# A graph layer on one core: results 13 steps behind their group instead of 17, dense stores issued by ScalarE, and 4/9 of a step in each lookup turn

## The chip, the cores and the metric

The kernel runs on one core of a Trainium2 chip. The time is the device time of one execution in microseconds (us); of several runs the median is given. A profile of one execution shows what each engine did: TensorE (PE, its weight loads PEld), VectorE (DVE), ScalarE (ACT), GpSimd (POOL) and SyncE (SP), whose queue (SPq) only issues transfers here. All transfers share the core's DMA engines.

## The reference

One graph layer on 100,000 nodes of 128 numbers with 25,000 edges, followed by a layer norm over all nodes. Only nodes that own an edge get anything beside `x + x`.

```python
# src, dst: 25000 node numbers each; the layer's own dst is src, its src is dst
edge_feat = concatenate([h[dst], h[src], rel_pos, distance], axis=-1)
x = silu(edge_feat @ W1 + b1)
x = silu(x @ W2 + b2)
scores = (x @ W3 + b3)[:, 0]
mx = segment_max(scores, dst); exp_scores = exp(scores - mx[dst])
den = segment_sum(exp_scores, dst)
alpha = exp_scores / (den[dst] + EPS)
msg = h[src] @ Wv * (alpha * node_weight[src])[:, None]
out = segment_sum(msg, dst)
return layernorm(x + (h + out))
```

## The kernel before

The work has a dense and a sparse side.

**Dense.** All 100,000 rows are normalised as if no node had an edge. They come in 98 blocks of 1024 rows (`xin`, a ring of 8 blocks of 512 KB), two in each turn: SP loads a block (`load_block`, L323, which waits until the block that held the place has been stored), DVE takes its statistics (L969) at the end of a turn, a chain of 11 small DVE operations after every second turn (L930 to L951) makes scale and bias for four blocks, two turns later ACT (L510, 7 of a block's 8 rows per partition) and DVE (L990, the eighth) apply them, and SP stores the block (`store_block`, L332, after both).

**Sparse.** The edges are sorted by owner first (until about 105 us), then they are worked in 49 groups of 512. For 43 of them a lookup on PE finds sender and edge features of each sorted place (24 matmuls, L713, then 8 small ones, L700, between which DVE picks with L1018); the other 6 are fetched by GpSimd. GpSimd issues all indirect transfers in a fixed order, four for each piece: owner rows (`hk`), records of the 6 groups (`rt`), sender rows (`rec`, L443 for all), and last the scatters of the finished results (L447). The first scatter waits for all dense stores (`dense_written`, at turn 53), since a scatter overwrites dense rows; the scatter of a group waits for its result (`res_ready`, ACT L559). Sender rows pass through `rec` (a ring of `HS_RING` groups), are written out by SP (`write_rec`, L347) and come back by `load_rec` (L353) as `region`; the gather of group g waits until the group that held its place has been written out.

**Order.** Everything is written out by hand as turns, numbered from 0. Turns 0 to 42 hold one lookup each; turns 0 to 51 also hold dense work. A step s has three parts on each engine; it moves up to 18 groups one stage on: group s is transposed, s-1 meets `W1`, s-2 meets `W2`, s-3 is scored, and after the softmax of a batch of 4 groups its weights (`M_LAG`), sums (`Z_LAG`), rows (`Y_LAG`) and results follow. From turn `E_FROM` on each lookup turn takes one part of a step, later turns take a whole step. So step 11 begins in turn 43, and there are 99 turns for 67 steps. `bank[6]` of PSUM is shared: PE's small transpose (L665) waits for ACT's copy of the senders (L520). After the last turn edges that cross a tile are mended (`fix`), with two last scatters (L451).

Of the kernel before, what the change touches and what calls it, by code (L numbers as in the profile page):

```python
# [12 lines left out]
P = 128  # L13
# [14 lines left out]

HS_RING, R_RING, X_RING = 4, 12, 8
HK_SEMS, SC_SEMS, Y_SEMS, FAR_RING = 16, 8, 4, 4  # L30
KROW_RING = 2
ACT_ROWS = 7

BATCH = 4
BT = BATCH * TPG
NBATCH = -(-G // BATCH)
Y_LAG, Z_LAG, M_LAG, KROW_LAG = 12, 10, 9, 8
LAST_STEP = 67

# [5 lines left out]
REC_LAG = 7  # L45
E_FROM = 10
PARTS = 3
# [27 lines left out]
def turn_plan():  # L75

    plan, left, turn = [], [(s, p) for s in range(LAST_STEP) for p in range(PARTS)], 0
    while left:
        now = []
        if E_FROM <= turn < LOOKS:  # L80
            now.append(left.pop(0))
        elif turn >= LOOKS:
            now.append(left.pop(0))
            while left and left[0][0] == now[0][0]:
                now.append(left.pop(0))
        plan.append(now)
        turn += 1
    return plan
# [5 lines left out]
def looks(g):  # L94

    return sum(1 for v in LOOKED if v <= g)


# [15 lines left out]
def gnn_kernel(nc, x, xw, rec5, snd_tab, ef_tab, rcv_nat, id_nat, signs, iota, rowid, colid, word, w16d, w1, b1, w2, b2, w3, b3,  # L114
# [11 lines left out]
    with ExitStack() as ctx:  # L126
# [171 lines left out]
        def chain_turn(b):  # L298
            return batch_end(b) + Y_LAG + 1

        def res_turn(g):
            return max(chain_turn(batch_of(g)) + 1 + g % BATCH, g + Y_LAG + BATCH + 1)


        @block.sync
        def _(sp):
# [13 lines left out]
            def load_block(j):  # L320
                if 0 <= j < NB:
                    wait_ring(sp, stored, j - X_RING, 16)
                    sp.dma_start(xin[:, j % X_RING], x[rows_of(j), :].rearrange("(p r) h -> p r h", p=P)  # L323
                                 ).then_inc(x_in[j % X_RING], 16)

            def store_block(j):
                if 0 <= j < NB:
                    wait(sp, "norm_a", j + 1)
                    wait(sp, "norm_d", j + 1)
                    if j == NB - 1:  # L330
                        wait_ring(sp, stored, j - 1, 16)
                    sp.dma_start(out[rows_of(j), :].rearrange("(p r) h -> p r h", p=P), xin[:, j % X_RING]  # L332
                                 ).then_inc(stored[j % X_RING], 16)

# [51 lines left out]

            for i, now in enumerate(TURNS):
                store_block(2 * (i - 3) + 1)
                if i + 1 < LOOKS:
                    load_places(i + 1)  # L390
                for g in range(G):
                    if looks(g) - 1 + REC_LAG == i:
                        write_rec(g)
                if i == E_FROM - 1:
# [16 lines left out]
                if i >= 3:  # L411
                    load_block(2 * (i + 1))
                store_block(2 * (i - 2))
                if i >= 3:
# [88 lines left out]
        def _(act):  # L503
            def norm(i, half):
                j = 2 * (i - 2) + half
                if 0 <= j < NB:
                    wait(act, "chain_d", (j // 4 + 1) * STEPS)
                    for n in range(ACT_ROWS):
                        c = j % 4 * BR + n
                        ins = nc.scalar.activation(xin[:, j % X_RING, n, :], xin[:, j % X_RING, n, :], ACT.Identity,  # L510
                                                   bias=drs[:, j // 4 % 2, 1, c:c + 1], scale=drs[:, j // 4 % 2, 0, c:c + 1])
                    ins.then_inc(S["norm_a"], 1)
# [13 lines left out]
            def hidden(s):  # L526
# [7 lines left out]
                for b in range(NBATCH):  # L534
                    if batch_end(b) + 4 == s:
# [4 lines left out]
            def results(s):  # L540
                g = s - Z_LAG
# [4 lines left out]
                for b in range(NBATCH):  # L546
                    if batch_end(b) + 5 == s:
                        n = group_tiles(b)
                        wait(act, "alphaT_done", b + 1)
                        wait(act, "acol_ready", b - 1)  # L550
                        nc.scalar.activation(alT[:, b % 2, 0:n], bank[6][:, 0:n], ACT.Copy).then_inc(S["alT_ready"], 1)
                for g in range(G):
                    if res_turn(g) == s:
# [7 lines left out]
                        ins.then_inc(S["res_ready"], 1)  # L561

            for i, now in enumerate(TURNS):
                norm(i, 0)
                for s, part in now:
                    (turned, hidden, results)[part](s)
                norm(i, 1)

# [10 lines left out]
        def _(pe):  # L579
# [79 lines left out]
            def small_turns(s):  # L659
# [6 lines left out]
                for b in range(NBATCH):  # L666
                    if batch_end(b) + 5 == s:
# [23 lines left out]
            def turns(s):  # L691
                if s + 1 < G:
                    turn_rows(s + 1)
                    turn_senders(s + 1, sum(batch_end(b) + 5 <= s for b in range(NBATCH)))

# [45 lines left out]
        def _(dve):  # L741
# [220 lines left out]
            def dense_stats(i):  # L962
# [10 lines left out]
                if i % 2 == 1 or i == NPAIR - 1:  # L973
# [3 lines left out]
                    def gate():  # L977
                        wait(dve, "norm_a", 4 * (k - 1))
                        wait(dve, "norm_d", 4 * (k - 1))

# [3 lines left out]
            def dense_norm(i):  # L984
                for j in (2 * (i - 2), 2 * (i - 2) + 1):
                    if 0 <= j < NB:
                        wait(dve, "chain_d", (j // 4 + 1) * STEPS)
                        for n in range(ACT_ROWS, BR):
                            c = j % 4 * BR + n
# [102 lines left out]
            def part_two(s):  # L1092
                for b in range(NBATCH):
                    if chain_turn(b) == s:
                        def gate(b=b):
                            wait(dve, "res_ready", batch_end(b - 2) + 1 if b >= 2 else 0)

                        running.append(chain(("y_stats", batch_end(b) + 1), group_tiles(b), est[:, b % 2], ers[:, b % 2], cwe,
                                             "chain_e", b * STEPS, gate))
                    if batch_end(b) + 4 == s:  # L1100
                        softmax_first(b)
                    if batch_end(b) + 6 == s:
                        wait(dve, "alT_ready", b + 1)
# [4 lines left out]
                        dve.wait_ge(S["acol_ready"], b + 1)  # L1108

            def part_three(s):  # L1110
                if 0 <= s - M_LAG < G:
                    weights(s - M_LAG)
                more(3)
                for b in range(NBATCH):
                    if batch_end(b) + 4 == s:
                        softmax_second(b)
                more(99)
                if s == batch_end(NBATCH - 1) + 5:
                    dve.sem_inc(S["parts_ready"], 1)

            for i, now in enumerate(TURNS):
                if 0 <= i - 1 < LOOKS:
                    take_places(i - 1)
                one_hot(i, 0, EARLY)
                for b in range(NBATCH):
                    if (batch_end(b) + 4, 0) in now:
                        take_scores(b)
                if 0 <= i - 1 < LOOKS:
# [118 lines left out]
```

## Time and profile before

| | us |
|---|---|
| median of 3 runs (1011.95 to 1016.06) | 1012.76 |
| the profiled execution | 1010.98 |
| its span | 1009.2 |

The page of the profile gives the share of the span in which each engine was busy: PE 73%, DVE 65%, POOL 59%, ACT 52%, weight loads 49%. TensorE's clock was granted 0.892 of full on the mean. The profile moved 188.47 MB, mean 187 GB/s. The busy shares are means over very different stretches: sorting with DVE alone to about 105 us, lookups with dense work to about 562 us, steps with dense work to about 665 us, steps alone, and a tail of scatters. An engine's line says how long it was busy and who ended its idle time; for SP only its queue's waits are known. The program takes 1.78 us beyond its span.

### The profile page before, as it was taken

The numbers are of one execution on the slowest core, as the hardware profiler recorded it, in microseconds if no ns is written. First come the engines' busy times: TensorE is split into PE (matmuls) and PEld (weight loads), VectorE is DVE, ScalarE is ACT, GpSimd is POOL, SyncE is SP. The second block draws the span as 40 slices with busy tenths as digits, with TensorE's granted clock in tenths as the row PEclk, the third lists the DMA queues.
The fourth block names the chain that finished last, engine by engine and source line by source line (L and its number), as shares of the span: only waits on it lengthen the run. The fifth ranks groups of instructions, "written<-read, shape, count | busy, mean of one in ns | idle before, by whom it ended". The sixth has DMA issues, their size and how long they took to land.

```text
span 1009.2 us, 13449 instructions
## 1 busy us (share of the span) xinstructions
PE 735.5 (73%) x3718; PEld 493.6 (49%) x3718; DVE 655.5 (65%) x2314; ACT 527.1 (52%) x1230; POOL 596.9 (59%) x624
## 2 busy tenths in 40 slices
PE   0001688889878878797889786799999999996700
PEld 0000355555555545564556454566766666665600
DVE  8988789877766757676787666544355535547741
ACT  0000066566555645555556576876566666664630
POOL 3000777777777777777774337717644444446677
PEclk9999988989987878888898988899999999998755
DMA  6000369999889979979999869533322222222131
GB/s 215 0 0 5 78 186 315 336 344 344 288 269 320 327 217 331 329 223 291 356 321 321 247 208 304 168 117 101 92 80 83 80 83 85 83 65 66 65 80 45
DMA packets 120371, 188.47 MB, mean 187 GB/s; under 512 B 21147, under 2 KB 80182, under 8 KB 120296
## 3 DMA queue, kind: packets, MB, share of 16 engines
q1 hardware_dynamic: 100648, 148.85, 45.5%
q0 software_dynamic: 19648, 38.74, 13.8%
q8 instruction: 31, 0.51, 0.2%
q14 instruction: 44, 0.36, 0.1%
HBM read 109.89 MB, written 77.76 MB: 186 GB/s over the span
## 4 chain that ended last, share of the span: by engine, by line
PE 41%; DVE 19%; POOL 15%; issue 8%; DMA 8%; ACT 6%; SPq 2%; POOLq 0%; DVEq 0%; ACTq 0%
PE bank L713 9%; POOL rec L443 6%; POOL hk L443 6%; PE bank L680 4%; PE bank L687 4%; PE bank L643 4%; PE bank L655 4%; PE bank L634 3%; DMA xin<-in_x 3%; POOL out_rows L447 3%; PE bank L652 3%; PE bank L653 3%; ACT xin L510 3%; DVE region L776 3%; PE bank L700 2%
## 5 line engine op out<-in xcount | busy, mean ns | idle before, releaser
L510 ACT ACTIVATE xin<-xin,drs 128x128 f32<-128x128 f32 x686 | 269.4, 480 | 268.8 <-DVE drs L951 268.8
L447 POOL DMA_INDIRECT out_rows<-hk,sidx_t x196 | 192.4, 982 | 155.6 <-ACT hk L559 83.8
L713 PE MATMUL bank<-hk 128*125 128x512 bf16 x1032 | 267.5, 422 | 8.3 <-DVE snd_i L1026 5.4
L443 POOL DMA_INDIRECT hk<-in_x,kg_t x196 | 186.4, 951 | 143.5 <-DVE kg_t L860 84.0
L443 POOL DMA_INDIRECT rec<-in_xw,snd_i x196 | 185.5, 947 | 96.3 <-issue 56.7
L713 PEld LDWEIGHTS bank<-hk 128*125 128x125 bf16 x1032 | 156.7, 154 | 115.1 <-issue 40.6
L969 DVE BATCH_NORM_STATS2 dst<-xin 128x6 f32<-128x256 f32 x392 | 135.6, 413 | 32.8 <-DMA xin<-in_x 32.5
L1011 DVE TENSOR_SCALAR hk<-hk,rid 128x512 bf16<-128x512 f16 x344 | 110.0, 381 | 0.5 <-DMA hk<-vc_d 0.3
L1078 DVE TENSOR_TENSOR hk<-bank,hk 128x512 f32<-128x512 f32 x49 | 33.6, 687 | 102.1 <-PE bank L680 102.1
L700 PE MATMUL bank<-wsel,hk 125*128 125x5 f32 x344 | 52.4, 276 | 59.1 <-DVE hk L1018 59.1
L700 PEld LDWEIGHTS bank<-wsel,hk 125*128 125x128 f32 x344 | 48.6, 218 | 73.2 <-DVE hk L1018 71.7
L559 ACT ACTIVATE hk<-hk,ers 128x128 f32<-128x128 f32 x196 | 79.5, 482 | 0.4 <-DVE ers L951 0.4
L530 ACT ACTIVATE x<-bank,bcol 128x512 f32<-128x512 f32 x49 | 33.6, 686 | 66.5 <-PE bank L655 66.5
L586 PE MATMUL bank<-ident,region 128*128 128x128 f32 x8 | 2.7, 445 | 86.8 <-DVEq L792 86.8
L655 PEld LDWEIGHTS bank<-efT,w 16*128 16x128 f32 x392 | 47.2, 186 | 37.2 <-issue 37.2
L680 PE MATMUL bank<-wvh,zs 128*128 128x128 f32 x392 | 59.6, 300 | 6.8 <-ACT zs L545 3.4
L545 ACT ACTIVATE zs<-bank 128x512 f32<-128x512 f32 x49 | 29.0, 591 | 64.7 <-PE bank L687 64.7
L1069 DVE TENSOR_SCALAR m_q<-krow,kcol,acol 128x128 f32<-128x128 bf16 x196 | 57.1, 348 | 7.4 <-DMA krow<-seg_d 6.4
L1018 DVE SCALAR_TENSOR_TENSOR hk<-hk,cid,bank 125x512 f32<-125x512 f16 x43 | 31.9, 742 | 44.7 <-PE bank L713 44.7
L643 PE MATMUL bank<-x,w2s 128*128 128x512 f32 x98 | 60.9, 706 | 0.0
L687 PE MATMUL bank<-m_q,region 128*128 128x128 f32 x392 | 57.8, 296 | 0.0
L680 PEld LDWEIGHTS bank<-wvh,zs 128*128 128x128 f32 x392 | 52.6, 208 | 9.6 <-ACT zs L545 6.0
(203 smaller groups left out, 1020.7 us busy)
## 6 DMA issues: line engine op xcount, KB each, us to landing
xin<-in_x SPq DMA_DIRECT2D x98, 512.0 KB, 6.8
out_rows<-xin SPq DMA_DIRECT2D x98, 512.0 KB, 7.5
rec_d<-rec SPq DMA_DIRECT2D x49, 258.0 KB, 5.6
region<-rec_d SPq DMA_DIRECT2D x49, 258.0 KB, 3.4
hk<-vc_d SPq DMA_DIRECT2D x43, 256.0 KB
krow<-seg_d SPq DMA_DIRECT2D x49, 128.0 KB, 3.3
hk<-in_x,kg_t POOLq DMA_INDIRECT x196, 5.5
rec<-in_xw,snd_i POOLq DMA_INDIRECT x196, 6.0
```

The costliest lines, as they stand in the source:

```text
L443: pool.indirect_dma_start(out=to, out_offset=None, in_=frm, in_offset=bass.IndirectOffsetOnAxis(ap=index, axis=0)).then_inc(done, 16)
L447: pool.indirect_dma_start(out=out, out_offset=bass.IndirectOffsetOnAxis(ap=index, axis=0), in_=frm, in_offset=None).then_inc(done, 16)
L510: ins = nc.scalar.activation(xin[:, j % X_RING, n, :], xin[:, j % X_RING, n, :], ACT.Identity, bias=drs[:, j // 4 % 2, 1, c:c + 1], scale= ...
L559: ins = nc.scalar.activation(hk[:, g, q, :], hk[:, g, q, :], ACT.Identity, scale=ers[:, b % 2, 0, n:n + 1], bias=ers[:, b % 2, 1, n:n + 1])
L643: pe.matmul(bank[2][:], w2s[:], x1[:], start=True, stop=True).then_inc(S["mm2_done"], 1)
L655: ins = pe.matmul(bank[1][:, q * P:(q + 1) * P], w16[:, q, :], efT[:, g % 2, :], start=False, stop=(q == TPG - 1), skip_group_check=True)
L680: ins = pe.matmul(bank[4][:, q * P:(q + 1) * P], zs[:, q * P:(q + 1) * P], wvh[:], start=True, stop=True)
L687: ins = pe.matmul(bank[5][:, q * P:(q + 1) * P], rr[:, g % R_RING, q, 0:H], m_q[:, g % 2, q, :], start=True, stop=True)
L700: ins = pe.matmul(bank[7][:, q * WORDS:(q + 1) * WORDS], sel[0:SEL, q * P:(q + 1) * P], wsel[0:SEL, :], start=True, stop=True)
L713: ins = pe.matmul(bank[7][0:SEL, :], tab[:, k, n, 0:SEL], oh[:, k, :], start=(k == 0 and n == 0), stop=(k == CH - 1 and n == PIECES - 1))
L969: ins = vec.bn_stats(dst[:, c:c + 2, :].rearrange("p j w -> p (j w)"), xin[:, j % X_RING, n:n + 2, :].rearrange("p j h -> p h j"))
L1011: ins = vec.tensor_scalar(pair(oh[:, k, :]), vt[:, u % 2, :, 0, :], rid[:, k:k + 1], None, ALU.is_equal)
```

## The change

- `ACT_ROWS = 7` goes; `act_rows(j)` gives ACT all 8 rows of the blocks that are normalised in lookup turns (blocks 0 to 81) and 5 of the others (82 to 97); DVE does the rest, so none in lookup turns. The counts that wait for DVE's rows follow (`shared`).
- The dense stores move from SP to ACT's queue (`store`): the odd block's after ACT's first half of the next turn, the even block's after the turn's parts.
- SP writes the records out (`write_rec`) in turn g+7, behind the first of the turn's two block loads, no longer in turn looks(g)+6 at its beginning; `HS_RING` is 6, not 4.
- Steps begin in turn 9, and every third lookup turn takes two parts. 45 parts (15 steps) lie in lookup turns where 33 (11 steps) lay; step 15 begins in turn 43; 88 turns in all for 60 steps.
- All lags behind a group's scores are two steps shorter, softmax and what follows it one step earlier; the results come 13 steps behind their group, not 17, those of the last two batches at once.

```diff
-HS_RING, R_RING, X_RING = 4, 12, 8
+HS_RING, R_RING, X_RING = 6, 12, 8
-ACT_ROWS = 7
-Y_LAG, Z_LAG, M_LAG, KROW_LAG = 12, 10, 9, 8
-LAST_STEP = 67
+Y_LAG, Z_LAG, M_LAG, KROW_LAG = 10, 8, 7, 6
+LAST_STEP = 60
-E_FROM = 10
+E_FROM = 9
         if E_FROM <= turn < LOOKS:
             now.append(left.pop(0))
+            if (turn - E_FROM) % PARTS == PARTS - 1:
+                now.append(left.pop(0))
+def act_rows(j):
+    return BR if j // 2 + 2 < LOOKS else 5
+def shared(j):
+    return sum(1 for k in range(j + 1) if act_rows(k) < BR)
...
-            return batch_end(b) + Y_LAG + 1
+            return batch_end(b) + Y_LAG
...
-            return max(chain_turn(batch_of(g)) + 1 + g % BATCH, g + Y_LAG + BATCH + 1)
+            return chain_turn(batch_of(g)) + (g % BATCH if batch_of(g) < NBATCH - 2 else 0)
...
             for i, now in enumerate(TURNS):
-                store_block(2 * (i - 3) + 1)
                 if i + 1 < LOOKS:
                     load_places(i + 1)
-                for g in range(G):
-                    if looks(g) - 1 + REC_LAG == i:
-                        write_rec(g)
...
                 if i >= 3:
                     load_block(2 * (i + 1))
-                store_block(2 * (i - 2))
+                if 0 <= i - REC_LAG < G:
+                    write_rec(i - REC_LAG)
                 if i >= 3:
                     load_block(2 * (i + 1) + 1)
...
+            def store(j):
+                if 0 <= j < NB:
+                    wait(act, "norm_a", j + 1)
+                    wait(act, "norm_d", shared(j))
+                    if j == NB - 1:
+                        wait_ring(act, stored, j - 1, 16)
+                    act.dma_start(out[rows_of(j), :].rearrange("(p r) h -> p r h", p=P), xin[:, j % X_RING]
+                                  ).then_inc(stored[j % X_RING], 16)
             for i, now in enumerate(TURNS):
                 norm(i, 0)
+                store(2 * (i - 3) + 1)
                 for s, part in now:
                     (turned, hidden, results)[part](s)
+                store(2 * (i - 2))
                 norm(i, 1)
```

SP, in a lookup turn that also loads records for a step (`hk<-vc_d` opens the turn, `rec_d<-rec` is `write_rec`, `region<-rec_d` is `load_rec`), first of the kernel before:

```order
204 L341 DMA hk<-vc_d 128x1024
205 L347 DMA rec_d<-rec 128x4x129 x2
206 L353 DMA region<-rec_d 128x4x129
207 L323 DMA xin<-in_x 128x1024
208 L332 DMA out_rows<-xin 128x1024
209 L323 DMA xin<-in_x 128x1024
210 L332 DMA out_rows<-xin 128x1024
```

and of the changed one:

```order
155 L343 DMA hk<-vc_d 128x1024
156 L355 DMA region<-rec_d 128x4x129
157 L379 DMA krow<-seg_d 128x512
158 L334 DMA xin<-in_x 128x1024
159 L349 DMA rec_d<-rec 128x4x129
160 L334 DMA xin<-in_x 128x1024
```

The record writes stand behind the first block load, and no store stands in SP's queue.

ACT, over two to three lookup turns in the middle (`xin<-xin,drs` are dense rows, the others belong to steps), before:

```order
66 L510 ACTIVATE xin<-xin,drs 128x128 x14
67 L551 ACTIVATE alT<-bank 128x16
68 L510 ACTIVATE xin<-xin,drs 128x128 x14
69 L518 ACTIVATE hkT<-bank 128x512
70 L520 ACTIVATE hsT<-bank 128x512
71 L524 ACTIVATE x<-bank,bcol 128x512
72 L510 ACTIVATE xin<-xin,drs 128x128 x14
```

and now:

```order
107 L568 DMA out_rows<-xin 128x1024
108 L509 ACTIVATE xin<-xin,drs 128x128 x16
109 L568 DMA out_rows<-xin 128x1024
110 L517 ACTIVATE hkT<-bank 128x512
111 L519 ACTIVATE hsT<-bank 128x512
112 L523 ACTIVATE x<-bank,bcol 128x512
113 L568 DMA out_rows<-xin 128x1024
```

Between two parts there are 16 dense rows instead of 14, and two issues of stores in each turn, the odd block's behind 8 rows of the next.

ACT at the end of the turns (`hk<-hk,ers` makes results, 4 rows for each group), before:

```order
416 L559 ACTIVATE hk<-hk,ers 128x128 x4
417 L545 ACTIVATE zs<-bank 128x512
418 L559 ACTIVATE hk<-hk,ers 128x128 x4
419 L545 ACTIVATE zs<-bank 128x512
420 L559 ACTIVATE hk<-hk,ers 128x128 x32
```

and now:

```order
523 L558 ACTIVATE hk<-hk,ers 128x128 x4
524 L550 ACTIVATE zs<-bank 128x512
525 L558 ACTIVATE hk<-hk,ers 128x128 x4
526 L550 ACTIVATE zs<-bank 128x512
527 L558 ACTIVATE hk<-hk,ers 128x128 x24
```

Six groups' results stand behind the last sums, where eight stood.

## Rows read from the trace of the kernel before

**Rows 1.** Busy time by stretch: stretch, length, then each engine, clock, DMA share, GB/s

```profile
190.50:562.00 371.50, 315.44 (x1412) 203.43 (x1413) 265.97 (x923) 214.42 (x532) 272.30 (x288) 0.87 0.95 307
562.00:640.00 78.00, 55.27 (x293) 38.34 (x291) 53.10 (x186) 50.69 (x116) 40.10 (x43) 0.82 0.78 230
```

**Rows 2.** The chain that ended last, its end: start, length, what

```profile
964.44 0.97 POOL out_rows L447
...
1005.24 1.00 POOL out_rows L451
```

**Rows 3.** GpSimd's waits, whole span: total, times, longest

```profile
POOL out_rows L447 <- ACT hk L559: 83.8, 28, 4.3
```

**Rows 4.** GpSimd by line: shortest/median/longest ns, first and last start

```profile
L443 POOL DMA_INDIRECT hk<-in_x,kg_t x196: 940/944/1136, 99.4 to 656.0; - x196
L447 POOL DMA_INDIRECT out_rows<-hk,sidx_t x196: 963/969/1147, 677.8 to 1004.0; - x196
```

**Rows 5.** GpSimd in order of time, one gather: start, length, [pause before it <-releaser]

```profile
603.44 0.94 POOL L443 DMA_INDIRECT rec<-in_xw,snd_i  x1 [0.30 <-issue]
```

**Rows 6.** Waits of SP's own queue, whole span, and of DVE for blocks (190 to 562)

```profile
SPq L347 <- DMA rec<-in_xw,snd_i: 132.1, 31, 8.6
SPq L323 <- DMA out_rows<-xin: 43.7, 31, 2.9
DVE dst L969 <- DMA xin<-in_x: 30.6, 18, 3.2
```

**Rows 7.** SP's queue in order of time, one lookup turn

```profile
430.76 6.31 SPq L347 DMA_DIRECT2D rec_d<-rec  x2
...
437.67 0.54 SPq L323 DMA_DIRECT2D xin<-in_x  x1
```

**Rows 8.** DVE in order of time, the first one-hots of turn 9

```profile
190.48 0.99 DVE L1011 TENSOR_SCALAR hk<-hk,rid 128x512 bf16<-128x512 f16 x3
```

**Rows 9.** PE in order of time, a lookup and what follows

```profile
407.49 5.39 PE L713 MATMUL bank<-hk 128*125 128x512 bf16 x24 [0.21 <-DVE snd_i L1026]
416.96 1.87 PE L700 MATMUL bank<-wsel,hk 125*128 125x5 f32 x8 [4.08 <-DVE hk L1018]
```

**Rows 10.** The chain, steps alone: transposes of two steps, rows and sums between

```profile
880.66 0.44 PE bank L615 x4
...
886.58 0.89 PE bank L680 x8
887.47 0.89 PE bank L687 x8
888.36 0.44 PE bank L615 x4
```

**Rows 11.** PE in order of time, the W1 product of steps 21 and 49

```profile
679.12 1.02 PE L652 MATMUL bank<-hkT,w1a 128*128 128x512 f32 x2
...
908.36 1.02 PE L652 MATMUL bank<-hkT,w1a 128*128 128x512 f32 x2
```

**Rows 12.** DVE in order of time: softmax of turn 43, dense rows of turn 44

```profile
569.73 0.41 DVE L1055 TENSOR_TENSOR_SCAN soft<-cont,soft 16x128 f32<-16x128 bf16 x1 [3.33 <-ACT soft L538]
...
577.34 0.60 DVE L990 TENSOR_SCALAR xin<-xin,drs 128x128 f32<-128x128 f32 x2
```

**Rows 13.** In order of time: ACT's dense rows of turn 44, then PE's small transpose

```profile
577.34 2.80 ACT L510 ACTIVATE xin<-xin,drs 128x128 f32<-128x128 f32 x7 [4.47 <-DVE drs L951]
...
581.25 0.37 PE L665 MATMUL bank<-ident,efs 128*16 128x128 f32 x1 [6.34 <-ACT hsT L520]
```

**Rows 14.** Transfers by line, size, median us to landing; then the store's issue, ns

```profile
xin<-in_x SPq DMA_DIRECT2D x98, 512.0 KB, 6.8
out_rows<-xin SPq DMA_DIRECT2D x98, 512.0 KB, 7.5
rec_d<-rec SPq DMA_DIRECT2D x49, 258.0 KB, 5.6
L332 SPq DMA_DIRECT2D out_rows<-xin x98: 337/394/1785, 131.2 to 663.2; - x98
```

More of the change, by code:

```diff
@@ L324, in load_block @@
                                  ).then_inc(x_in[j % X_RING], 16)
[L326 to L333, printed above, removed]
             for j in range(X_RING):
@@ L507, in norm @@
                     wait(act, "chain_d", (j // 4 + 1) * STEPS)
-                    for n in range(ACT_ROWS):
+                    for n in range(act_rows(j)):
                         c = j % 4 * BR + n
@@ L534, in hidden @@
                 for b in range(NBATCH):
-                    if batch_end(b) + 4 == s:
+                    if batch_end(b) + 3 == s:
                         n = group_tiles(b)
@@ L540, in results @@
             def results(s):
+                for b in range(NBATCH):
+                    if batch_end(b) + 4 == s:
+                        n = group_tiles(b)
+                        wait(act, "alphaT_done", b + 1)
+                        wait(act, "acol_ready", b - 1)
+                        nc.scalar.activation(alT[:, b % 2, 0:n], bank[6][:, 0:n], ACT.Copy).then_inc(S["alT_ready"], 1)
                 g = s - Z_LAG
@@ L545, in results @@
                     nc.scalar.activation(zs[:], bank[5][:], ACT.Copy).then_inc(S["zs_ready"], 1)
[L546 to L551, printed above, removed]
                 for g in range(G):
@@ L666, in small_turns @@
                 for b in range(NBATCH):
-                    if batch_end(b) + 5 == s:
+                    if batch_end(b) + 4 == s:
                         n = group_tiles(b)
@@ L693, in turns @@
                     turn_rows(s + 1)
-                    turn_senders(s + 1, sum(batch_end(b) + 5 <= s for b in range(NBATCH)))
+                    turn_senders(s + 1, sum(batch_end(b) + 4 <= s for b in range(NBATCH)))
             def words(u):
@@ L978, in gate @@
                         wait(dve, "norm_a", 4 * (k - 1))
-                        wait(dve, "norm_d", 4 * (k - 1))
+                        wait(dve, "norm_d", shared(4 * (k - 1) - 1))
                     n = (2 * i + 2 - 4 * k) * BR
@@ L985, in dense_norm @@
                 for j in (2 * (i - 2), 2 * (i - 2) + 1):
-                    if 0 <= j < NB:
+                    if 0 <= j < NB and act_rows(j) < BR:
                         wait(dve, "chain_d", (j // 4 + 1) * STEPS)
-                        for n in range(ACT_ROWS, BR):
+                        for n in range(act_rows(j), BR):
                             c = j % 4 * BR + n
@@ L1099, in part_two, with part_three @@
                                              "chain_e", b * STEPS, gate))
+                    if batch_end(b) + 3 == s:
+                        take_scores(b)
+                        softmax_first(b)
+            def part_three(s):
+                for b in range(NBATCH):
                     if batch_end(b) + 4 == s:
-                        softmax_first(b)
-                    if batch_end(b) + 6 == s:
                         wait(dve, "alT_ready", b + 1)
@@ L1114, in part_three @@
                 for b in range(NBATCH):
-                    if batch_end(b) + 4 == s:
+                    if batch_end(b) + 3 == s:
                         softmax_second(b)
                 more(99)
-                if s == batch_end(NBATCH - 1) + 5:
+                if s == batch_end(NBATCH - 1) + 3:
                     dve.sem_inc(S["parts_ready"], 1)
@@ L1124, in _ @@
                 one_hot(i, 0, EARLY)
-                for b in range(NBATCH):
-                    if (batch_end(b) + 4, 0) in now:
-                        take_scores(b)
                 if 0 <= i - 1 < LOOKS:
```

1 line of the change is left out of this document (removed).

## The prediction

> **What bounds the kernel now.** I read the busy time by stretch first, then the chain that ended last, GpSimd's waits and lines, SP's own queue, and last single turns of PE, DVE and ACT.
>
> The chain ends on GpSimd: the last wait for a result in it is over at 964.44, and from there scatters follow each other without a pause to the two `fix` scatters at 1005.24; the span ends 4.0 us later [rows 2]. 32 scatters lie between, 1.275 us each (40.8 / 32). All 196 need 249.9 us, yet they take 327.4, from 677.8 to 1005.24 [rows 2, 4]: GpSimd waits 83.8 us for results in between [rows 3]. It waits because in the middle stretch a step takes 8.19 us on PE (679.12 to 908.36 are 28 steps [rows 11]) and brings one group, whose four scatters take 5.1. So two engines set the end by turns, PE through the steps and GpSimd at the tail. If the results were there in time, GpSimd alone would end the span at **S0 + 249.9 + 4.0**, where S0 is its first scatter. S0 has two conditions: the dense stores (now 677.8) and the end of its own gathers, whose last is issued at 656.0 [rows 4]. One gather takes 1.24 to 1.25 us with its pause [rows 5], so four make 5.0 and the ten last owner groups, which can't be fetched before the lookups leave their memory, 50.1.
>
> Before that, the lookup turns: turn 9 begins its one-hots at 190.48 [rows 8] and turn 43 begins near 562, where turn 42's lookup ends: 34 turns of 10.93 us, which are the first stretch of rows 1. PE works 315.4 of 371.5 us there, at a mean clock of 0.87 [rows 1]. The rest are pauses like 4.08 us before the small matmuls, which wait for DVE [rows 9], and DVE is late because it waited 30.6 us for blocks [rows 6]. The blocks are late because SP stands: 132.1 us in 31 waits for gathered senders in `write_rec` [rows 6], 6.31 us in the turn shown, with the block load only behind it at 437.67 [rows 7]. Then turns 43 to 48 take 78 us, 13 each [rows 1].
>
> **The change part by part.**
>
> *Lookup turns.* Four more steps lie in them. A step is 7.70 us on PE (880.66 to 888.36 [rows 10]). Rows and sums (L680, L687) take 1.8 of it in the chain [rows 10], say 2.0 with the lower clock; before, one of 11 steps had sums, now seven of 15 have. So PE gets 15 x 7.70 - 8 x 2.0 = 99.5 us of step work where it had 11 x 7.70 - 10 x 2.0 = 64.7: 35 us more in 34 turns, **+1.0 us per turn**. Against it: PE's idle time is 56 us in this stretch now (371.5 - 315.4), 1.6 per turn [rows 1]; DVE loses both eighth rows of the turn, 0.60 us [rows 12], and the SP stall that caused most of the block waits, 0.9 us per turn (30.6 / 34), goes: `write_rec` for group g comes in turn g+7, up to six turns later, when its gather is done for 20 us and more. A lookup takes 5.39 us at the upper clock [rows 9] and the more so the more pauses there are, so fewer pauses also give a little back. I set the two sides equal: the lookup turn stays 10.9 us, **turn 43 stays at 562**. From below the turn is bounded by PE's work without pauses, 5.39 + 1.0 (1.87 at the lower clock [rows 9]) + 4/9 x 7.70 = 9.8 us; with 0.6 of pauses, 10.4 (turn 43 at 544). From above by no relief at all, 11.9 (turn 43 at 595).
>
> *ACT.* 16 rows in a turn for 14: seven take 2.80 us [rows 13], so +0.8, and two issues of stores, 0.39 us each by SP's rows [rows 14], +0.8. ACT has 214.4 us of work in 371.5 [rows 1], 6.5 per turn, so it comes to 8.1 and with its 1/9 step (under 0.5) to 8.6 of 10.9. On the path: nothing, as long as PE's copies, which stand behind 8 dense rows, are wanted a turn later only. The odd block's store now waits behind 8 rows of the next turn, 3.2 us. Store 7.5, load 6.8 [rows 14], 3.2 and an issue of 0.8 make 18.3, against some two turns less the statistics, 20: covered, with under 2 us to spare. SP waited 43.7 us for stores already [rows 6]; that is why I give nothing more to the gain.
>
> *Turns 43 to 48.* Two of these six turns take some 18 us now. In turn 43 softmax, statistics and chain stand in one DVE turn: DVE waits 3.33 for ACT's exponentials [rows 12], ACT's rows of turn 44 wait 4.47 for the chain and PE's small transpose 6.34 for ACT [rows 13]. The softmax falls three steps after a batch now, in even turns (46 and 50), the chain stays in odd ones, so this pile-up goes. Also `load_rec` waits for a sum three steps back instead of one. DVE gets 6 dense rows per turn for 2 (+1.3), so about 9.7 us per turn: 53.1 us in six turns [rows 1] are 8.9, less 0.5 for one softmax of some 3 us that leaves them, plus 1.3. I take 10.5: **turn 49 at 562 + 63 = 625**. Bounds 9.3 and 13.0 (as now).
>
> *GpSimd's gathers.* With `HS_RING` 6 the last sender gather (group 48) waits for group 42's record write, in turn 49. It lands 5.6 us after its issue [rows 14]; 5.0 for its four gathers and 50.1 for the owners: **S0 = 625 + 5.6 + 55.1 = 686**. That is 8 us later than now, though turn 49 is earlier, since the write stands four turns later in turn count. The stores are done by turn 53, 625 + 4 x 9.7 = 664: not binding.
>
> *The scatters.* End of the span 686 + 249.9 + 4.0 = **940**, if no result is late. The result of group g comes at the end of step g+13, step 26 begins in turn 54 at about 673. With 8.19 per step: group 13 at 681, group 35 at 861; GpSimd reaches group 35 at 686 + 35 x 5.1 = 864. So twelve results stand ready at S0, and the lead lasts just to the end of the full steps (862). Behind them nine short steps remain to the results of the last two batches, where 17 remained: from 908 to 964 they took 3.5 us each; with the two softmaxes of 7.7 inside it the nine take about 45, so group 44 at 907 and GpSimd there at 910. Both paths give 940; as the larger of two near ones, 941. The 83.8 us of waiting [rows 3] go, and that is the gain.
>
> The profiled execution lies 1.8 us above its span; 941 + 1.8 = **943** against 1010.98, 6.7% less. The median of before lies another 1.8 above (0.2%), which I leave out.
>
> *A page of the notes.* Rows 7 show SP held for 6.31 us with a load behind it, so a queue's stall costs here. The Trainium skill (DMA: Bandwidth & Descriptors, section "Issuing engines are not separate DMA queues") says transfers of all issuing engines share the same DMA engines and another issuer saves only issue time. By that, with the share of 0.95 in rows 1, the stores' move would give no bandwidth; what the trace adds is that the in-order waits, not the issue time, were the cost.
>
> **The rivals.**
>
> *Bandwidth bounds the lookup turns.* The DMA share is 0.95 at 307 GB/s [rows 1]. Then a turn can't shrink when SP is freed, and the larger share of a step adds 1/9 of 387 KB (258 of records [rows 14], 128 of keys by the page), 0.14 us. With a third of PE's added work beside it: 11.4 us, turn 43 at 578, turn 49 at 641, span 956, time **958**. Against it: SP's stall leaves holes in which no load is under way [rows 7], and the share counts packets that wait.
>
> *The ring of blocks bounds.* If the odd block's store behind 8 rows makes the loads late and ACT at 8.6 us falls behind, the lookup turn goes to 12.0 and turns 43 to 48 to 11.5: 190.5 + 408 + 69 = 667, span 982, time **984**.
>
> *All goes better.* Lookup turn 10.4, later turns 9.3: turn 49 at 600, S0 661, span 915, time **917**.
>
> *Slower than before.* ACT becomes the pace: it works its queue in order, so rows, PE's products and the chain's end are waited for one behind the other. With 8.6 of work, one wait for a product (3 us) and half the chain's wait (4.47 / 2 [rows 13]) a turn is 13.8: turn 43 at 660, turn 49 at 738, span 1053, time 1054. It decides from a turn 49 at 695 on (695 + 60.7 + 253.9 = 1009), which with 13.0 for the six turns is 12.5 per lookup turn.
>
> *It doesn't shorten what it says:* sums and scatters again in step with a slow PE, within 0.5%: only if the extra steps cost in the lookups just what they save, 12.4 per turn; I find no row for it.
>
> **How the numbers follow.** Forecast 0.52 (943, its own spread 928 to 958), bandwidth 0.15, better 0.15, ring 0.13, slower 0.04, no change 0.01. The range holds the forecast, bandwidth, most of "better" and of the ring case, so it runs from 914 to 984. Faster by over 0.5% (about what a measurement can tell from no change) 0.95, the same 0.01, slower 0.04.
>
> **What would show it.** Right: SP has no long waits in `write_rec`; turn 43 at 550 to 575 with PE's clock near 0.9; the last sender gather in turn 49 near 630; first scatter near 686 and GpSimd without waits for results until the end. Wrong: DVE still waits 30 us for blocks, or ACT's copies are what PE waits for (turn 43 past 590); the gathers of the last senders waiting beyond turn 50; waits for results over 20 us in total, which would say that the steps, not GpSimd, set the end.

## The result and the profile after

The changed kernel takes 929.75 us (median of 4 runs, 929.4 to 930.98) against 1014.41 for the kernel before in the same comparison: ratio 0.9166, 95% interval 0.9134 to 0.9197. It is 8.3% faster; 943 was forecast, 914 to 984 the range. The profiled execution takes 929.5 with a span of 927.7; every trace read below is of one execution.

| where (by the traces) | before | forecast | after |
|---|---|---|---|
| turn 43 begins on PE | 561.4 | 562 | 537.0 |
| turn 49 begins on PE | 639.6 | 625 | 606.7 |
| last sender gather begins | 602.2 | 631 | 608.5 |
| first scatter | 677.8 | 686 | 663.8 |
| GpSimd's waits for results | 83.8 | 0 | 11.6 |
| last group's scatters begin | 1000.2 | 931 | 918.7 |

The page, costliest groups (line, engine, shapes; busy us, mean ns; idle before them and who ended it). These are the blocks' statistics, the lookup and the small matmuls behind it:

```profile
span 927.7 us, 13366 instructions
...
L723 PE MATMUL bank<-hk 128*125 128x512 bf16 x1032 | 247.4, 400 | 7.3 <-DVE snd_i L1036 4.5
...
L979 DVE BATCH_NORM_STATS2 dst<-xin 128x6 f32<-128x256 f32 x392 | 135.1, 410 | 7.0 <-DMA xin<-in_x 7.0
...
L710 PE MATMUL bank<-wsel,hk 125*128 125x5 f32 x344 | 46.9, 260 | 35.6 <-DVE hk L1028 35.6
```

DVE waited 7.0 us for blocks; in the stretch of the lookup turns it was 30.6 [rows 6]. Busy time by stretch (PE, PEld, DVE, ACT, POOL, clock, DMA share, GB/s), lookup turns 9 to 42 and turns 43 to 48, which answer to [rows 1]:

```profile
187.00:541.00 354.00, 322.02 (x1638) 213.75 (x1638) 268.91 (x930) 265.31 (x647) 262.53 (x276) 0.95 0.98 323
541.00:607.00 66.00, 55.98 (x278) 40.88 (x278) 53.83 (x192) 47.52 (x112) 25.01 (x27) 0.82 0.90 262
```

PE is idle for 32 us of the lookup turns where it was for 56, at a clock of 0.95 where it was 0.87, and it does four more steps in the stretch. SP's queue in order of time, one lookup turn, against [rows 7]:

```profile
410.59 0.32 SPq L343 DMA_DIRECT2D hk<-vc_d  x1
411.02 0.41 SPq L334 DMA_DIRECT2D xin<-in_x  x1
411.48 0.43 SPq L349 DMA_DIRECT2D rec_d<-rec  x1
414.38 0.33 SPq L334 DMA_DIRECT2D xin<-in_x  x1
```

The record write takes 0.43 us and holds nothing up. The pause before the last load is the wait for a store that ACT issues now, the odd block's behind 8 dense rows. Such waits of SP add up to 128.4 us over the span, where they were 43.7 [rows 6], but DVE hardly feels them.

GpSimd by line (shortest/median/longest ns, first and last start), its waits for results, and the end of the chain, against [rows 2 to 4]:

```profile
L442 POOL DMA_INDIRECT hk<-in_x,kg_t x196: 940/944/1569, 99.0 to 662.6; - x196
L446 POOL DMA_INDIRECT out_rows<-hk,sidx_t x196: 963/969/1152, 663.8 to 922.5; - x196
```

```profile
POOL out_rows L446 <- ACT hk L558: 11.6, 8, 3.4
```

```profile
922.49 0.97 POOL out_rows L446
...
923.77 1.00 POOL out_rows L450
```

The last owner gather is issued at 662.6 and the first scatter at 663.8: GpSimd goes from one into the other, as the forecast said, and from there to 923.77 it takes 260.0 us where 249.9 is the least. The last long pause in between:

```profile
872.77 0.96 POOL L446 DMA_INDIRECT out_rows<-hk,sidx_t  x1 [3.35 <-ACT hk L558]
```

From there on scatters follow each other to the end. So what the end hangs on is still a late result, that of group 39, and not the first scatter.

### The profile page after: what moved, and what is told of

Its sections match the earlier page's. It is cut to its first block, busy times and chain, and to the rows that moved or that the text cites. A ratio compares the mean times of both kernels' runs of the same rounds, so it can differ in the third digit from the quotient of the medians.

```text
span 927.7 us, 13366 instructions
## 1 busy us (share of the span) xinstructions
PE 707.7 (76%) x3718; PEld 485.4 (52%) x3718; DVE 640.9 (69%) x2264; ACT 548.5 (59%) x1280; POOL 597.2 (64%) x624
## 4 chain that ended last, share of the span: by engine, by line
PE 42%; DVE 23%; POOL 11%; DMA 9%; issue 8%; ACT 5%; SPq 1%; ACTq 0%; DVEq 0%; POOLq 0%
PE bank L723 13%; POOL out_rows L446 11%; DMA xin<-in_x 6%; DVE dst L979 4%; PE bank L710 3%; PE bank L665 3%; PE bank L653 3%; PE bank L697 3%; PE bank L690 3%; DMA out_rows<-xin 3%; ACT xin L509 3%; DVE region L786 3%; PE bank L662 3%; PE bank L663 3%; PE bank L644 3%
## 5 line engine op out<-in xcount | busy, mean ns | idle before, releaser
L509 ACT ACTIVATE xin<-xin,drs 128x128 f32<-128x128 f32 x736 | 290.2, 480 | 198.0 <-DVE drs L961 192.0
L723 PE MATMUL bank<-hk 128*125 128x512 bf16 x1032 | 247.4, 400 | 7.3 <-DVE snd_i L1036 4.5
L446 POOL DMA_INDIRECT out_rows<-hk,sidx_t x196 | 191.0, 975 | 68.9 <-issue 57.3
L723 PEld LDWEIGHTS bank<-hk 128*125 128x125 bf16 x1032 | 147.3, 145 | 99.2 <-issue 21.7
L710 PE MATMUL bank<-wsel,hk 125*128 125x5 f32 x344 | 46.9, 260 | 35.6 <-DVE hk L1028 35.6
L710 PEld LDWEIGHTS bank<-wsel,hk 125*128 125x128 f32 x344 | 43.5, 198 | 47.4 <-DVE hk L1028 46.2
L690 PE MATMUL bank<-wvh,zs 128*128 128x128 f32 x392 | 62.4, 310 | 4.3 <-ACT zs L550 3.4
L697 PE MATMUL bank<-m_q,region 128*128 128x128 f32 x392 | 62.2, 311 | 0.0
L1079 DVE TENSOR_SCALAR m_q<-krow,kcol,acol 128x128 f32<-128x128 bf16 x196 | 59.0, 358 | 1.8 <-PE bank L697 1.1
L690 PEld LDWEIGHTS bank<-wvh,zs 128*128 128x128 f32 x392 | 55.3, 216 | 7.3 <-ACT zs L550 4.6
L697 PEld LDWEIGHTS bank<-m_q,region 128*128 128x128 f32 x392 | 58.3, 228 | 0.1
```

The source lines that it names most:

```text
L446: pool.indirect_dma_start(out=out, out_offset=bass.IndirectOffsetOnAxis(ap=index, axis=0), in_=frm, in_offset=None).then_inc(done, 16)
L690: ins = pe.matmul(bank[4][:, q * P:(q + 1) * P], zs[:, q * P:(q + 1) * P], wvh[:], start=True, stop=True)
L697: ins = pe.matmul(bank[5][:, q * P:(q + 1) * P], rr[:, g % R_RING, q, 0:H], m_q[:, g % 2, q, :], start=True, stop=True)
L710: ins = pe.matmul(bank[7][:, q * WORDS:(q + 1) * WORDS], sel[0:SEL, q * P:(q + 1) * P], wsel[0:SEL, :], start=True, stop=True)
L723: ins = pe.matmul(bank[7][0:SEL, :], tab[:, k, n, 0:SEL], oh[:, k, :], start=(k == 0 and n == 0), stop=(k == CH - 1 and n == PIECES - 1))
L1079: ins = vec.tensor_scalar(m_q[:, g % 2, q, :], krow[:, g % KROW_RING, q * P:(q + 1) * P], kcol[:, t:t + 1], acol[:, b % 2, n:n + 1], ALU.i ...
```

## The experiments

Times are medians of four executions (five in one case); since not all ran beside the same runs, they are compared by their ratio to the kernel before (the changed kernel: 0.9166). The trace is of one of the executions, which can lie some us from the median: 9 us under it in experiment 1, 8 us over it in the first run of experiment 3, 6 us under it in the first of experiment 5, 7 us under it in the first of experiment 6. Differences of a few us between two traces are to be read with that in mind. "A lookup turn" is the distance from turn 9's lookup to turn 42's, divided by 33: 10.96 us before, 10.40 in the changed kernel.

**1. The record writes alone.** The kernel before with one edit:

```diff
-HS_RING, R_RING, X_RING = 4, 12, 8
+HS_RING, R_RING, X_RING = 6, 12, 8
-                for g in range(G):
-                    if looks(g) - 1 + REC_LAG == i:
-                        write_rec(g)
...
+                if 0 <= i - REC_LAG < G:
+                    write_rec(i - REC_LAG)
                 store_block(2 * (i - 2))
```

> The kernel before with one part of the change: record writes in turn g+7 behind the first block load, ring of 6; stores, rows, lags and share of a step stay as before. Theory (SP's stall in the record writes was what made the lookup turns long): SP waits under 15 us there in lookup turns instead of 132, DVE waits for blocks under 12 us instead of 30.6, turn 43 begins 25 to 35 us earlier, and since steps on PE set what follows, the time falls by as much: 975 to 990. Rival (the stores in ScalarE's queue or the dense rows did it): less than 10 us, 1003 or more.

978.3 us, ratio 0.9697 (0.9647 to 0.9747). Turn 43 begins at 520.7, 41 us earlier than before and more than expected (the trace is of the fastest execution, 969.35); a lookup turn takes 9.83 us for 10.96. SP's wait in `write_rec`, which was 132.1 [rows 6]:

```profile
SPq L347 <- DMA rec<-in_xw,snd_i: 4.2, 4, 1.6
```

DVE's wait for blocks in the lookup turns, then GpSimd's for results:

```profile
DVE dst L968 <- DMA xin<-in_x: 1.6, 2, 1.3
```

```profile
POOL out_rows L446 <- ACT hk L558: 56.2, 20, 4.4
```

The theory holds: without SP's stall in the record writes the time is 33 us less, with the stores still in SP's queue and the rows shared as before. The edit also makes the ring 6 instead of 4, but experiment 7 takes the ring back to 4 and its turn 43 is not later (530.0 for 537.0), so it is not the ring. Whether the later turn or the place behind the block load did it, this run doesn't tell. PE does the same work in these 34 turns (1411 matmuls here, 1412 before). It was busy for 315.4 us of 371.5 and is for 295.9 of 333.9, so its idle time falls by 18 us and its busy time by 19.5, at a mean granted clock of 0.93 for 0.87. GpSimd still waits 56 us for results. The DMA share is 1.00 at 328 GB/s from 186 to 540 us (before: 0.95 at 307), and nobody waits for a block for more than 1.3 us, so bandwidth was not what made the turns long.

**2. The stores back on SP.** The changed kernel with `store_block` on SP at its old places and no `store` on ACT:

```diff
             for i, now in enumerate(TURNS):
+                store_block(2 * (i - 3) + 1)
                 if i + 1 < LOOKS:
                     load_places(i + 1)
...
+                store_block(2 * (i - 2))
                 if 0 <= i - REC_LAG < G:
...
-                store(2 * (i - 3) + 1)
...
-                store(2 * (i - 2))
```

> The changed kernel with the dense stores back in SP's queue, at the places they had before (the odd block's at the turn's start, the even one's behind the first load). Theory (the record writes did it, the stores little): 0 to 8 us slower than the changed kernel, 930 to 938. Rival (SP's wait for ScalarE's rows, 61.7 us before, held the loads as well): turn 43 15 us or more later, 945 or more.

924.0 us, ratio 0.9116 (0.9053 to 0.9178): not slower, as had been expected, if anything faster; the intervals overlap. SP's waits in it, the one for ACT's rows:

```profile
SPq L343 <- ACT xin L520: 119.7, 46, 10.9
```

SP waits 119.7 us for ACT's rows (61.7 before the change), and moving that wait out of SP's queue gains nothing. With the stores on ACT, SP waits longer for the stores to land instead, 128.4 us for 77.3 here. So not every wait of the queue matters: this one stands before a store whose place a later load needs anyway. The Trainium skill (DMA: Bandwidth & Descriptors, section "Issuing engines are not separate DMA queues") says that another issuing engine only saves the time of the issue. The traces agree: in the lookup turns the DMA share is 0.98 either way, at 327 GB/s here and 323 in the changed kernel.

**3. Rows 7 and 1, stores on ACT, then on SP.**

```diff
 def act_rows(j):
-    return BR if j // 2 + 2 < LOOKS else 5
+    return 7
```

> The changed kernel with the dense rows shared 7 and 1 in all blocks as before. Theory (PE paces the lookup turns, DVE and ScalarE have room): within 5 us of the changed kernel; DVE 0.6 us more per lookup turn, 1.3 less in turns 43 to 51, where DVE was expected to be the tightest, so turns 43 to 48 take 66 us for 70 and turn 43 comes 0 to 5 us later. Rival (DVE paces the lookup turns): 0.6 us x 34 = 20 us later in turn 43, 945 or more.

945.2 us, ratio 0.9347 (0.9315 to 0.938): the expectation of "within 5" missed. In its trace, the slowest execution of the five, turn 43 comes 12 us later, of which 6 stand before turn 9 already, and the ten turns from 43 on take 122 us (549.2 to 671.3) for 111. The trace showed ACT waiting 35.2 us for DVE's rows ahead of its stores, which led to a second theory, and that to a run with the same edit and the stores on SP:

> The changed kernel with the stores on SP and the rows shared 7 and 1 in all blocks, both as before. With the stores on ScalarE the 7 and 1 cost 15 us, and ScalarE waited 35 us there for VectorE's rows ahead of its stores. Theory (the cost of 7 and 1 is that wait in ScalarE's in-order queue, not VectorE's own time): with the stores on SP it is gone, 921 to 931. Rival (VectorE's 0.6 us per lookup turn is what costs): 938 or more.

941.0 us, ratio 0.9307 (0.9269 to 0.9345), 17 us slower than experiment 2. The new theory fell too. The time lies where the rival put it, but not for the rival's reason: a lookup turn takes 10.36 us for 10.29 in experiment 2, not 0.6 more. The turns 43 to 52 take 119.4 us for 107.8 in experiment 2, though DVE has less to do in them (busy 69.4 us for 77.2), while ACT is busy for 93.3 us and for 81.9 there. ACT in order of time in two of these turns:

```profile
564.18 5.48 ACT L520 ACTIVATE xin<-xin,drs 128x128 f32<-128x128 f32 x14
569.56 0.57 ACT L528 ACTIVATE hkT<-bank 128x512 f32<-128x512 f32 x1
...
573.94 0.60 ACT L561 ACTIVATE zs<-bank 128x512 f32<-128x512 f32 x1 [2.04 <-PE bank L706]
574.44 1.64 ACT L569 ACTIVATE hk<-hk,ers 128x128 f32<-128x128 f32 x4
575.98 5.48 ACT L520 ACTIVATE xin<-xin,drs 128x128 f32<-128x128 f32 x14
```

From one line of 14 rows to the next are 11.8 us, of which ACT pauses 2.0; PE waits for its copies. PE's wait in this stretch, first here, then in experiment 2:

```profile
PE bank L684 <- ACT hsT L530: 18.9, 8, 2.9
```

```profile
PE bank L684 <- ACT hsT L530: 9.3, 7, 1.4
```

So with seven rows ACT, not DVE, is the tight engine where a whole step meets dense rows: 5.5 us of rows and some 5 us of a step's work.

**4. Seven rows in lookup turns, five behind them**, stores on SP. It tells the two halves of that edit apart:

```diff
 def act_rows(j):
-    return BR if j // 2 + 2 < LOOKS else 5
+    return 7 if j // 2 + 2 < LOOKS else 5
```

> Stores on SP; ScalarE does 7 rows of a block in lookup turns and 5 in turns 43 to 51 (VectorE 1 and 3). 7 and 1 throughout cost 17 us against 8 then 5: by the traces 6 of them to turn 43 and 12 in the nine turns behind it. Theory (ScalarE is the tight engine of turns 43 to 51, where it does a whole step beside the rows; the eighth row in lookup turns matters little): turn 43 up to 6 us later, the ten steps behind it again 108 us, time 924 to 931. Rival (the lookup turns' row is what costs, the rest is scatter of runs): 937 or more.

928.7 us, ratio 0.9148 (0.9103 to 0.9193). The ten turns take 106.4 us (537.6 to 644.0), as short as in experiment 2; turn 43 is 5 us later. Of the 0.019 that 7 and 1 cost in ratio, 0.016 come back with the 5 rows alone. That ACT does all 8 in lookup turns is worth 0.003, about 3 us; the intervals don't tell that from nothing.

**5. A third of a step in each lookup turn, then half of one.**

```diff
-            if (turn - E_FROM) % PARTS == PARTS - 1:
-                now.append(left.pop(0))
```

> The changed kernel with one part (1/3 of a step) in each lookup turn instead of 4/9. Lookup turns get shorter, four steps more follow behind them at 8.2 us. Theory (a step's part costs PE time in the lookup turn, some of it hidden in pauses): lookup turn 9.5 to 9.9 for 10.3, turn 43 some 15 to 27 us earlier, 33 us of steps added: 6 to 18 us slower, 936 to 948. Rival (the extra part is hidden wholly, the turn has another bound): the turn stays 10.3 and the time rises by 33, to 962.

947.0 us, ratio 0.937 (0.9338 to 0.9402): 0.020 of the gain is the four further steps in the lookup turns. A lookup turn takes 9.86 us for 10.40, so a ninth of a step costs 0.54 us in it, where it saves 8.2 / 9 = 0.91 behind it. Turn 43 comes 11 us earlier, less than the 15 to 27 expected, and GpSimd waits 42.2 us for results where it waited 11.6. The other direction, with the stores on SP:

```diff
-            if (turn - E_FROM) % PARTS == PARTS - 1:
+            if (turn - E_FROM) % 2 == 1:
```

> Stores on SP (924 so far) and half a step in each lookup turn instead of 4/9, so 17 steps lie in lookup turns. Theory (the part costs PE time in the turn, and GpSimd's start hangs on turn 49 by its number, not by its step): turn 43 later by 10 to 15 us, the steps behind it end within 4 us of where they did, but the first scatter comes 10 to 15 us later: 928 to 938. Rival (the part is hidden in pauses): turn 43 within 4 us, time 918 to 924.

927.9 us, ratio 0.9145 (0.9109 to 0.9181), no gain over experiment 2. Turn 43 is 7 us later, less than the 10 to 15 expected. The last result comes at 871.2 for 881.9, but the first scatter at 669.7 for 668.3, and GpSimd, which waits for no result in either, ends as late. This is the plainest sign that its line is the bound once the stores are on SP; in the changed kernel itself it still waits 11.6 us for results.

**6. The lags.** The changed kernel with the old lags in all places, then the kernel before with the new ones alone:

```diff
-Y_LAG, Z_LAG, M_LAG, KROW_LAG = 10, 8, 7, 6
-LAST_STEP = 60
+Y_LAG, Z_LAG, M_LAG, KROW_LAG = 12, 10, 9, 8
+LAST_STEP = 67
```

> The changed kernel with the lags of before: results 17 steps behind their group, softmax four steps behind, 67 steps in all; stores, rows, writes and the share of a step as changed. Theory (results must be there in time for GpSimd, else the end follows the steps again): step 49 stays near 845, the last result comes 60 us behind it as before (905) and not 47; GpSimd waits for results over 30 us in total for 11.6, the time rises by 20 to 28: 950 to 958. Rival (GpSimd's start sets the end and the lags are hidden): under 938.

959.3 us, ratio 0.9492 (0.9447 to 0.9536); its profiled execution 952.4.

```profile
L446 POOL DMA_INDIRECT out_rows<-hk,sidx_t x196: 967/972/1152, 676.2 to 945.4; - x196
```

```profile
POOL out_rows L446 <- ACT hk L558: 22.0, 11, 3.9
```

The median is 1 us above the expected range, the make-up only half right: the waits for results are 22.0 us and not over 30, and the first scatter itself is 12 us later (676.2 for 663.8), because turn 43 is 5 us later, turns 43 to 48 take 73 us for 70, and SP issues the last record write at 615.2, where turn 49 begins, and no longer 4 us ahead of it.

> The kernel before with the new lags alone (results 13 steps behind, softmax three, 60 steps); lookup turns as before, 1/3 of a step in each. Theory: the full steps end at the same time (step 49 near 905), but the last result comes 47 us behind it and not 60, and GpSimd has written nearly all by then, where 41 us of scatters stood behind the last result: span 976 to 984, time 978 to 986. Rival (the lags only serve the changed lookup turns): within 8 us, 1003 or more.

991.3 us, ratio 0.9769 (0.9727 to 0.9811), 23 us less, the direction right, the size under what was expected. The last result comes 46 us behind the last full step's scores (904.6 to 950.6) as expected, but the five groups of the last two batches come at once there, and their scatters of 25 us and the mending follow. GpSimd waits 68.9 us for results:

```profile
POOL out_rows L447 <- ACT hk L559: 68.9, 25, 4.5
```

**7. The ring of 4.**

```diff
-HS_RING, R_RING, X_RING = 6, 12, 8
+HS_RING, R_RING, X_RING = 4, 12, 8
```

> The changed kernel with HS_RING 4 as before, so that the sender gather of group g waits for the write of group g-4, two turns later. Theory (the end is GpSimd's first scatter plus 250 us of scatters): last sender gather near 630 for 608.5, first scatter 682 to 688 for 663.8, no waits for results left, span 936 to 943, time 938 to 945. Rival (the steps on PE set the end): the time stays within 3 us, 927 to 933.

934.1 us, ratio 0.9227 (0.9168 to 0.9287), 4 us under the range expected. The interval overlaps that of the changed kernel, so the time alone doesn't decide. The trace shows the mechanism:

```profile
L446 POOL DMA_INDIRECT out_rows<-hk,sidx_t x196: 968/972/1083, 675.3 to 925.4; - x196
```

```profile
POOL out_rows L446 <- ACT hk L558: 0.6, 2, 0.3
```

The first scatter is 11.5 us later, not 20, as this execution's turn 43 came 7 us earlier (530.0); the wait for results is all but gone, and the 196 scatters follow each other over 250.1 us without a break. Here the end is the first scatter plus that. The span grows by 3.0 us only (930.7 for 927.7), as the changed kernel loses 10 us to late results that this one doesn't.

**8. Half of the scatters.** Two of each group's four are left out:

```diff
-                    for q in range(TPG):
+                    for q in range(2):
                         t = g * TPG + q
                         scatter(hk[:, g, q, :], sidx_t[:, t:t + 1], scattered[g % SC_SEMS])
```

> The changed kernel with two of the four scatters of each group left out (so half of the result rows are not written). It shows what bounds the end next to GpSimd. The last result is ready at 894 in the changed kernel; from there the mending of edges that cross a tile took until 918.9 in its trace, and its two scatters began at 923.8. Theory (GpSimd's line of scatters ends only 5 us behind the mending): 3 to 6 us less, 924 to 927. Rival (GpSimd is the only bound of the tail): its last scatter about 20 us earlier, time 910 or less.

923.2 us, ratio 0.9089 (0.9051 to 0.9126), 7 to 8 us less, a little more than expected. GpSimd in order of time, the first of the two last scatters:

```profile
917.80 0.99 POOL L450 DMA_INDIRECT out_rows<-xin,fixi  x1 [18.58 <-ACT xin L583]
```

With 125 us of scatters gone GpSimd only waits 18.58 us for the mending. In the changed kernel itself ACT's last results and the mending's last rows stand so:

```profile
886.09 7.80 ACT L558 ACTIVATE hk<-hk,ers 128x128 f32<-128x128 f32 x20 [0.91 <-DVE ers L961]
...
918.04 0.88 ACT L583 ACTIVATE xin<-xin,ers 128x128 f32<-128x128 f32 x2 [9.56 <-DVE ers L961]
```

The mending takes 25 us from the last result (893.9) to 918.9, and GpSimd's line ends 5 us behind it. So a third bound, the mending, lies right under the other two.

**9. A version that beats both.** Stores on SP and the record write one turn earlier:

```diff
-REC_LAG = 7
+REC_LAG = 6
```

> Stores on SP (924 so far) and the record write of group g in turn g+6, one turn earlier, so that the last sender gather and with it GpSimd's first scatter come one turn earlier. Theory (GpSimd's line sets the end, the mending of crossing edges is 5 to 10 us behind it): first scatter 655 to 660 for 668, time 914 to 919. Rival (the write now stands before its gather is done and SP waits again, as before the change): turn 43 over 10 us later, time 930 or more.

918.3 us, ratio 0.9047 (0.8999 to 0.9096), 1.3% under the changed kernel with no overlap of the intervals. Against experiment 2, from which it differs in the write's turn alone, the intervals overlap (0.9053 to 0.9178 there), so that the earlier write gains by itself rests on the trace:

```profile
L457 POOL DMA_INDIRECT out_rows<-hk,sidx_t x196: 964/970/1153, 656.0 to 911.9; - x196
```

```profile
POOL out_rows L457 <- ACT hk L569: 7.7, 6, 3.4
```

```profile
SPq L358 <- DMA rec<-in_xw,snd_i: 13.9, 10, 2.6
```

The first scatter comes at 656.0 for 668.3, one turn earlier. SP waits 13.9 us for gathered senders again, in ten pieces of at most 2.6, which costs no turn (turn 43 at 531.5 for 532.5).

## Why the prediction was right, and where it was off

*The end.* The prediction put it as S0 + 249.9 + 4.0, with the steps on PE near the same place. By the profile it is 663.8 + 249.9 + 4.0 = 917.7, and 927.7 was measured: of the 10 us between, 9 are between groups 33 and 39, where GpSimd met the results (its waits in all: 11.6). "The larger of two near ones" was given 1 us and needed 10. GpSimd's line came out 22 us shorter than forecast and the steps' path 12, so the steps set the end once more, through group 39. The experiments bear both paths out: the ring of 4 and half a step (GpSimd's line alone), the old lags (results late), and they add the third, the mending, which the prediction did not have.

*Lookup turns, the term that was mis-sized.* Forecast +1.0 us of PE work and -1.0 of pauses, so 10.9; measured 10.40, and turn 43 at 537 for 562 (3.6 us of that stand before turn 9, which began at 186.9 for 190.5). The ninth of a step cost 0.54 us and not 1.0 (experiment 5): over the 34 turns PE is busy for 20 us more and not for 35, and idle for 5 us less. The stall's end gave 1.13 us per turn (experiment 1: 10.96 to 9.83), near the 1.0 set against it, but half of that is PE's faster work and not its pauses, and to this the forecast gave "a little". The lookup's 1032 matmuls, the same work, took 267.5 us on the page before, 257.9 in experiment 1, 257.6 in the first run of experiment 5 and 247.4 in the changed kernel, 20 us less in all, at mean clocks in the lookup turns of 0.87, 0.93, 0.93 and 0.95. So the term that was mis-sized is what the higher clock gives back.

*ACT.* Its work in the lookup turns was forecast at 8.6 us with two issues of stores. Measured are 265.3 / 34 = 7.8 without issues, which the profile doesn't count as busy, and 0.34 each for two of them, 8.5 in all. (The 6.5 that it starts from should be 6.3, 214.4 / 34.) PE waits for it once there, for 2.2 us; the rival in which it sets the pace fell. The margin of "under 2 us" for the odd block's store held: DVE's block waits went down to 7.0. But the stores' move itself brought nothing (experiment 2).

*Turns 43 to 48.* Forecast 10.5 us each, measured 11.6 (537.0 to 606.7). The pile-up shrank: the two longest of these turns take 14.4 and 14.3 us, where they took 19.8 and 18.2. But DVE was taken for the tightest engine, and with 7 rows it is ACT (experiments 3 and 4). With 5 rows DVE is busier again (53.8 us of 66, ACT 47.5), yet what PE waits for is ACT's copies, in five of the six turns, and in turn 47 for one more of them, 9.3 us in all:

```profile
588.57 0.37 PE L675 MATMUL bank<-ident,efs 128*16 128x128 f32 x1 [1.87 <-ACT hsT L519]
591.25 0.26 PE L682 MATMUL bank<-ident,soft 16*128 16x16 f32 x1 [2.30 <-ACT efT L532]
```

*The last record write.* Forecast to land 5.6 us into turn 49; SP runs ahead of PE and issued it before:

```profile
602.76 0.57 SPq L349 DMA_DIRECT2D rec_d<-rec  x1
```

The gather began 5.8 us later at 608.5, 1.8 into the turn: the duration was right, its start 4 us late. Then 55.3 us to the first scatter, forecast 55.1.

*The sum of the misses.* Turn 43 -25, the six turns +7, the write -4: the first scatter at 664, not 686. The waits at the meeting of the two paths +9: the time 13.5 below the forecast. The order of the stages and what each hangs on was right: SP's stall, the last record write, the results. But the total is nearer than its parts, as misses of 29 us one way and 16 the other cancel in part, and that is luck. Of the signs named as "right", SP's waits in `write_rec` are gone; turn 43 (537, not 550 to 575), the last gather (608, not 630), the first scatter (664, not 686) and "without waits for results" (11.6) did not come as named. None of the signs named as "wrong" came either.

*Slips in the working.* From 908 to 964 the 17 short steps took 3.3 us each (56.1 / 17), not 3.5, and by the prediction's own times 14 results, not twelve, stand ready at S0. Neither moves its sum: from step 49's `W1` product to group 44's result 41 us went by, where 45 were forecast.

*The rivals.* Bandwidth: the share rose to 0.98 at 323 GB/s in the changed kernel and to 1.00 at 328 in experiment 1, with the blocks in time, so it did not bind. The ring of blocks: SP's wait for stores is there (128.4 us), but the loads came in time. "All goes better" had the right lookup turn (10.4) and the wrong later turns (9.3 for 11.6).

*Parts of the gain, each by its own run:* record writes 0.030 of the ratio (experiment 1), lags 0.023 alone and 0.033 in the changed kernel (experiment 6), the further ninth of a step 0.020, 5 rows in place of 7 behind the lookups about 0.016, the stores and the eighth row nothing that these runs can tell. They add up to 0.09 to 0.10 and not to 0.083, as each is worth more or less with the others there.

## What to carry to other kernels

In a queue that works in order, look for the wait with something urgent behind it: taking 132 us of SP's waits for gathered rows away gained 33 us, while moving 120 us of waits for rows ahead of stores to another queue gained nothing. When an engine that waits for work (here GpSimd, 84 us) becomes the bound, its earliest possible start counts, and that may hang on a turn's number in quite another queue. And where two or three paths end within some 10 us of each other, as scatters, results and mending do here, the sum should be made for all of them, with some us added for where they meet.

## What the runs showed of the hardware

The same 1032 lookup matmuls took 267.5 us at a mean granted clock of 0.87 in the stretch of lookup turns and 247.4 at 0.95, after PE's idle time there fell from 56 to 32 us. In experiment 1, with PE's work unchanged, 18 us less of idle time came with 19.5 us less of busy time. So in these runs a filled pause gave back about twice its own length; no run changes the clock alone. GpSimd's indirect scatters kept 1.28 us each over all 196 with steps and transfers around them (250.1 us from the first to the last in the run with the ring of 4).
